# Sorting a graph's edges by source in lanes of four instead of two, with nine of sixteen tiles picked on the tensor engine

## The chip, the cores and the metric

The kernel runs on one core of a Trainium2 chip. The metric is the device time of one execution in microseconds. The profile is of one execution on the same core.

## The reference, cut to what matters

There are 8192 nodes with 128 features and 262144 edges. An edge has a source `src` (uniform at random), a destination `dst`, a weight and nine attributes; the edges come sorted by `dst`, whose density falls with the node's number (`8192 * u ** 2`).

```python
def _L0_gnn_ref(x, edge_row, edge_col, edge_vals, W):      # src, dst, edge_weight
    gathered = x[edge_col] * edge_vals[:, None]
    pre_embed = jax.ops.segment_sum(gathered, edge_row, num_segments=N)
    return pre_embed @ W.T
...
x = _layernorm(x + _L0_gnn_ref(x, src, dst, edge_weight, L0_gnn_W), axis=-1)
x = _layernorm(x + _L1_gnn_ref(x, edge_index, edge_attr_9, ...), axis=-1)
```

The first layer reads rows of `x` at `dst` and sums them at `src`, so it goes against the order in which the edges come. The second layer reads at `src`, forms a tensor product with the nine attributes, and sums at `dst`, in the order given.

## The kernel before, in words

The edges are seen as 128 rows of 2048. Row r holds edges r * 2048 onward; it is laid into a lane (a partition) so that lanes 2c and 2c + 1 hold row c and row 127 - c (`constants`, L124). Five blocks of code follow each other, with all engines meeting between them.

**Setup** (`setup`, L201 to L481). The rows are loaded by three indirect transfers of POOL, which then clears the accumulator `acc` (L283). DVE casts source and destination to floats (L350), builds the sort key (source above destination, L354 to L357), and measures each lane's range of destinations; PE mirrors these ranges between the two lanes of a pair (L446). DVE then makes the tables of the second layer (`layer1_tables`, L294 to L341) and the node numbers that a pair can reach (`node_f`, L423 to L426).

**Sort** (`first_edges`, stages on DVE L773 to L817). Each lane sorts its 2048 keys by a network of compare stages. A stage is a maximum (L805), a comparison (L806), a minimum (L809) and two predicated copies that move the weights along (L814, L817), all on DVE; ACT saves the lower weights and moves the higher keys (L695, L699). Stages go down to distance 4 in four interleaved runs, then merge these down to distance `FINEST` = 2. Then the two lanes of a pair are merged once: SP swaps their keys and weights (L651, L654), DVE keeps the smaller keys in one lane and the larger in the other (L795 to L801), and four cleaning stages at distance 1024 to 128 follow. Odd lanes hold their keys negated. Meanwhile POOL gathers the rows of `x` that each pair can reach, ACT and PE split them into three bf16 parts (`split_step`, `keep_left`).

**First layer.** Each lane's sorted edges are 16 tiles of 128, 2048 tiles in all. Tile t of every pair is handled for one lane and then the other, in eight groups of eight tiles each: 256 groups. The loop runs over t, and its body holds 16 groups, written out. For each tile PE sums `rows^T @ hot` into PSUM, where `hot` (128 x `WIN0` = 360 nodes) has the edge's weight at its source, and the place of the 360 columns within 3 banks is a register loaded from `starts_row` (L1102). The rows come in two ways. In each group of eight, tiles 0, 2, 4 and 6 (`FETCHED`) are picked from the split rows held on chip: PE spreads the destinations over the partitions (`spread`, L1050), ACT copies them and makes `rest_hot` (L725 to L731), DVE makes `near_hot` (L894), PE multiplies three bf16 parts by `near_hot` and one by `rest_hot` (`fetch`, L1065, L1067), ACT copies the result to `msg` (L737). Tiles 1, 3, 5 and 7 are gathered by POOL straight from memory (L989) into a ring of 16 slots, at most four groups ahead. DVE makes the `hot` products (L902) and, when a half is done, adds its three banks to `acc` (L915). On PE the order of a step is written out by hand:

```python
spread(k + 2, ...)
fetch(k + 1, (j + 1) % GROUPS)
sums(k, w, t, s, j)
```

If a tile's sources span more than `WIN0`, or the starts of one tile number lie too far apart, or the destinations of a pair more than `SPAN`, a flag turns on and the loop runs over all nodes in windows instead (`n_pass`).

**Norm, second layer, norm** (`norm_stage`, `layer1`). In the second layer POOL gathers one tile of rows at a time (L1375) into a ring of 16, and the sums and products of PE and DVE follow it.

Of the kernel before, what the change touches and what calls it, by code (L numbers as in the profile page):

```python
# [36 lines left out]
P = 128  # L37
# [11 lines left out]
WIN0 = 360  # L49
BANKS = 3  # L50
STEP = 512 - WIN0
RUNS = 4
FINEST = 2
REACH = (BANKS - 1) * STEP + 512
NOWHERE = 16384.0
GROUP = 8
FETCHED = (0, 2, 4, 6)
GATHERS = (1, 3, 5, 7)
KIND = (0, 1, 0, 1, 0, 1, 0, 1)
FEATS = 16  # L60
GATHERED = 4
SUMMED0 = 18
SPAN = 160
# [3 lines left out]
PAIRS = P // 2  # L67
X_PAIRS = [c for c in range(PAIRS) if c % GROUP in FETCHED]
# [12 lines left out]
C_ROW = C_SWAP + P  # L81
C_UPPER = C_ROW + 1
C_SIGN = C_UPPER + 1
C_PLACE = C_SIGN + 1
C_WANTED = C_PLACE + 2
C_ALL = C_WANTED + 2

# [15 lines left out]
def constants(n_nodes):  # L103
# [22 lines left out]
    c[lane ^ 1, C_SWAP + lane] = 1.0  # L126
    c[:, C_ROW] = row
    c[:, C_UPPER] = lane % 2
    c[:, C_SIGN] = 1.0 - 2.0 * (lane % 2)
    spare = lane < 3 * (SPAN - P)  # L130
    c[:, C_PLACE] = lane
    c[:, C_PLACE + 1] = np.where(spare, P + lane % (SPAN - P), P)
    c[:, C_WANTED] = lane - CENTER
    c[:, C_WANTED + 1] = np.where(spare, P + lane % (SPAN - P) - CENTER, -1000)
# [7 lines left out]
def gnn_kernel(nc, x, src, dst, attr, weight, w_lin, w_tp, consts, out, tables, x1):  # L142
# [8 lines left out]
    with ExitStack() as ctx:  # L151
        def sb(name, shape, dt):
            return ctx.enter_context(nc.sbuf_tensor(name, shape, dt))

        g.cst = sb("cst", [P, C_ALL], F32)
        g.ident_bf = sb("ident_bf", [P, g.RN + 1], BF16)
        g.acc = sb("acc", [P, g.N + REACH], F32)
# [8 lines left out]
        g.mix = sb("mix", [P, NA, D], F32)  # L166
        g.dst_rel = g.dst_col
# [4 lines left out]
        with ExitStack() as mid:  # L172
# [6 lines left out]
            g.node_f = sm("node_f", [P, 2, PAIRS], F32)  # L179
# [21 lines left out]
def setup(nc, g, src, dst, weight, w_lin, w_tp, consts):  # L201

    RN, TN = g.RN, g.TN
    with ExitStack() as ctx:
# [17 lines left out]
        g.tile_start = sb("tile_start", [P, TN], F32)  # L222
        row_no = sb("row_no", [P, 1], I32)
        turn_bf = sb("turn_bf", [P, P], BF16)
        lanes = sb("lanes", [P, 2, 2], F32)
# [4 lines left out]
        shown_in = sb("shown_in", [P, 3, PAIRS], F32)  # L230
        w_scalar = sb("w_scalar", [P, MUL], F32)
        w_vec = [sb(f"w_vec{i}", [P, MUL], F32) for i in range(2)]
        off_f = sb("off_f", [P, TN], F32)
        word_f = sb("word_f", [P, TN // QUAD_TILES], F32)
# [18 lines left out]
        pool_turn = sem("setup_pool_turn")  # L253
# [5 lines left out]
        l1_step = sem("l1_step")  # L259
# [6 lines left out]
        def _(sp):  # L266
# [3 lines left out]
            loads = [(w_scalar, w0, w3), (w_vec[0], w1, w2), (w_vec[1], w1, w4)]  # L270
# [6 lines left out]
        def _(pool):  # L277
            pool.wait_ge(row_no_made, 1)
            pool.sem_inc(pool_turn, 1)
# [3 lines left out]
            nc.gpsimd.memset(g.acc[:], 0.0)  # L283

        @block.vector
        def _(dve):
# [6 lines left out]

            def layer1_tables(dve):  # L294

                TN, Q, R = g.TN, QUAD_TILES, ROW_TILES
                l1_steps = [0]

                def link(ins):

                    l1_steps[0] += 1
                    ins.then_inc(l1_step, 1)
                    dve.wait_ge(l1_step, l1_steps[0])
# [1241 lines left out]
```

## Time and profile before

| | us |
|---|---|
| median of 3 runs | 4782.76 (4782.1 to 4785.0) |
| the profiled execution, its own time | 4778.88 |
| its span, first to last instruction | 4777.1 |
| PE busy in the span | 3699.2 (77%) |
| POOL busy | 3114.5 (65%) |
| DVE busy | 2246.6 (47%) |
| ACT busy | 1123.9 (24%) |

The span has a clear order: setup to 60 us, sort to 489, first layer to 2101, norm to 2155, second layer to 4723, norm to the end. Shares over the whole span mix these. Times of rows are in microseconds from the span's start; a row of the timeline merges instructions of one kind that follow each other, with their count after the x. Matmuls are pipelined: their starts tell the pace, their durations overlap.

### The profile page before, as it was taken

How to read it: one execution, taken by the hardware profiler on the slowest of the kernel's cores; microseconds unless marked ns; L12 is line 12 of the kernel's file. 1: busy time of each engine (PE TensorE's matmuls, PEld its weight loads, DVE VectorE, ACT ScalarE, POOL GpSimd, SP SyncE). 2: the span in 40 equal slices, each digit the busy share in tenths (PEclk: the TensorE clock that was granted, in tenths of full speed). 3: DMA queues.
4: the chain of work that ended last, by engine and by line, in shares of the span. 5: the costliest groups of instructions: out<-in, count | busy, mean ns of one | idle time of the engine just before them, and what ended most of it. 6: DMA issues, size and time to landing. Idle time of an engine off the chain costs nothing. (4 is left out here: it accounts for less than half of the span.)

```text
span 4777.1 us, 70528 instructions
## 1 busy us (share of the span) xinstructions
PE 3699.2 (77%) x17795; PEld 2639.9 (55%) x17796; DVE 2246.6 (47%) x4407; ACT 1123.9 (24%) x1890; POOL 3114.5 (65%) x3160
## 2 busy tenths in 40 slices
PE   1210999999999999987777777777777777777775
PEld 1000666666666666665555555555555555555554
DVE  8999555555555555562333333333333333333334
ACT  2442433333333333341111111111111111111102
POOL 3300666666666666637777777777777777777773
PEclk6555999999999999986777777777777777777776
DMA  1000111111111111122222222222222222222223
GB/s 44 17 5 18 42 42 42 42 42 42 42 42 42 42 42 42 42 85 59 55 56 56 56 56 56 56 56 56 56 56 56 56 56 56 56 56 56 56 56 97
DMA packets 115386, 238.26 MB, mean 50 GB/s; under 512 B 54001, under 2 KB 54145, under 8 KB 114705
## 3 DMA queue, kind: packets, MB, share of 16 engines
q0 software_dynamic: 100784, 208.87, 16.4%
q1 hardware_dynamic: 9954, 20.54, 1.4%
q10 hardware_dynamic: 4608, 8.39, 0.5%
q8 instruction: 16, 0.26, 0.0%
q14 instruction: 24, 0.20, 0.0%
HBM read 227.09 MB, written 8.40 MB: 49 GB/s over the span
## 5 line engine op out<-in xcount | busy, mean ns | idle before, releaser
L1375 POOL DMA_INDIRECT feat<-x,ids x2048 | 1933.2, 944 | 636.5 <-issue 568.2
L989 POOL DMA_INDIRECT l_feat<-in_x,id_of x1024 | 1081.9, 1057 | 724.7 <-PE l_pre L1093 258.1
L1439 PE MATMUL quad<-attr_hot,feat 128*128 128x144 f32 x4096 | 990.8, 360 | 417.2 <-DMA feat<-x,ids 410.9
L1481 DVE TENSOR_TENSOR group<-group,quad 128x504 f32 (+1 forms) x512 | 348.0, 680 | 1685.6 <-PE quad L1439 1685.6
L1439 PEld LDWEIGHTS quad<-attr_hot,feat 128*128 128x128 f32 x4096 | 660.2, 215 | 743.5 <-issue 716.0
L1446 PE MATMUL mixed<-group,mix 128*128 128x192 f32 x2304 | 693.4, 487 | 130.7 <-DVE group L1481 130.7
L1446 PEld LDWEIGHTS mixed<-group,mix 128*128 128x128 f32 x2304 | 651.3, 306 | 175.0 <-DVE group L1481 175.0
L1399 ACT CAST ids<-src_col 128x8 int32 x256 | 50.5, 197 | 2288.8 <-DMA feat<-x,ids 2288.8
L894 DVE TENSOR_SCALAR near_hot<-place,cst 128x512 bf16<-128x512 bf16 x256 | 90.5, 353 | 666.2 <-ACT place L725 666.2
L725 ACT CAST place<-place_b 128x512 bf16<-128x512 f32 x256 | 149.8, 585 | 948.2 <-PE place_b L1050 948.2
L1467 DVE TENSOR_TENSOR attr_hot<-hot,attr_t 128x1152 f32<-128x1152 f32 x256 | 346.8, 1355 | 45.9 <-DVE hot L1461 22.4
L1093 PE MATMUL l_pre<-keys,msg 128*128 128x360 f32 x768 | 307.9, 483 | 0.1
L1093 PE MATMUL l_pre<-w_row,l_feat 128*128 128x360 f32 x768 | 295.1, 466 | 0.0
L1093 PE MATMUL l_pre<-pad,msg 128*128 128x360 f32 x768 | 295.1, 466 | 0.0
L902 DVE TENSOR_SCALAR w_row<-swap,src_of,w_of 128x360 f32<-128x360 f32 x640 | 264.8, 463 | 1.9 <-PE l_pre L1093 1.9
L1065 PE MATMUL got<-x_near,near_hot 128*128 128x128 bf16 x3072 | 257.3, 220 | 1.3 <-ACT rest_hot L731 0.8
L902 DVE TENSOR_SCALAR keys<-swap,src_of,w_of 128x360 f32<-128x360 f32 x640 | 252.1, 460 | 0.0
L902 DVE TENSOR_SCALAR pad<-swap,src_of,w_of 128x360 f32<-128x360 f32 x640 | 251.8, 459 | 0.0
L1431 PE MATMUL quad<-zero_bf 1*128 1x504 bf16 x512 | 204.2, 399 | 51.2 <-issue 49.5
L1067 PE MATMUL got<-x_rest,rest_hot 128*128 128x128 bf16 x1024 | 224.8, 220 | 0.0
L1065 PEld LDWEIGHTS got<-x_near,near_hot 128*128 128x128 bf16 x3072 | 215.4, 98 | 2.1 <-issue 1.9
L1395 ACT ACTIVATE group<-group 128x1728 uint32<-128x1728 uint32 x128 | 210.3, 1643 | 13.8 <-issue 13.8
(235 smaller groups left out, 3978.0 us busy)
## 6 DMA issues: line engine op xcount, KB each, us to landing
feat<-x,ids POOLq DMA_INDIRECT x2048, 2.5
l_feat<-in_x,id_of POOLq DMA_INDIRECT x1024, 2.7
attr_in<-in_edge_attr SPq DMA_DIRECT2D x129, 72.0 KB
norm_x<-in_x SPq DMA_DIRECT2D x16, 256.0 KB, 2.6
x<-norm_z ACTq DMA_DIRECT2D x16, 256.0 KB, 2.4
norm_x<-x SPq DMA_DIRECT2D x16, 256.0 KB, 2.7
out<-norm_z ACTq DMA_DIRECT2D x16, 256.0 KB, 2.4
l_feat<-in_x,node POOLq DMA_INDIRECT x64, 2.6
```

The lines of the kernel that those rows point to most:

```text
L902: made = nc.vector.tensor_scalar(hot_of[(j % 2) * GROUP + i], iota[KIND[i]], src_of[s][:, c:c + 1], w_of[s][:, c:c + 1], ALU.is_equal, ALU ...
L989: pool.indirect_dma_start(feat[:, slot, :], None, x, bass.IndirectOffsetOnAxis(ap=id_of[s][:, c:c + 1], axis=0)).then_inc(feat_in[slot], 16)
L1065: nc.tensor.matmul(to, near_hot[z][:, m * P:(m + 1) * P], x_near[:, a, part, :], start=(part == 0), stop=False)
L1067: last = nc.tensor.matmul(to, rest_hot[z][:, m * P:(m + 1) * P], x_rest[:, a, :], start=False, stop=True)
L1093: made = nc.tensor.matmul(pre[:, s, bass.ds(places[i], WIN0)], rows, hot_of[(j % 2) * GROUP + i], start=False, stop=(j == GROUPS - 1 and i ...
L1375: pool.indirect_dma_start(feat[:, t, :], None, x1, bass.IndirectOffsetOnAxis(ap=ids[t // H][:, t % H:t % H + 1], axis=0),).then_inc(feat_i ...
L1395: nc.scalar.memzero(group[z][:]).then_inc(group_zero, 1)
L1431: nc.tensor.matmul(quad[:, q, 0:NA * QUAD_WIN], zero_bf[0:1, 0:P], zero_bf[0:1, :], start=True, stop=False, skip_group_check=True)
L1439: nc.tensor.matmul(bank[:, :, bass.ds(off, WIN)], feat[:, t, :], attr_hot[t // H][:, t % H, :, :], start=False, stop=(t % Q == Q - 1), ski ...
L1446: last = nc.tensor.matmul(mixed[:, z, 0:GROUP_WIN], g.mix[:, m, :], group[z][:, m, :], start=(m == 0), stop=(m == NA - 1))
L1467: nc.vector.tensor_tensor(attr_hot[h][:], hot[:].unsqueeze(2).to_broadcast(s4), by_tile[:, h * H:h * H + H, :].unsqueeze(3).to_broadcast(s ...
L1481: nc.vector.tensor_tensor(to, to, quad[:, q, 0:NA * QUAD_WIN].rearrange("p (m n) -> p m n", m=NA), ALU.add).then_inc(quad_added, 1)
```

## The change

- **Lanes merged four by four.** `MERGED` = 4. After the pair merge and a sign flip (`C_FLIP`) nine cleaning stages (distance 1024 down to `CLEANEST` = 4) sort each lane again; then lane v meets lane 3 - v of its quad, and then lane 1 - v; the four cleaning stages 1024 to 128 stay. `FINEST` is 4, so the two stages at distance 2 go.
- **Spans of 184 columns.** `WIN0` is 184, and all starts of one tile number and lane lie within one bank of 512 columns, so `pre` is one bank per part, cleared once and added once. A part is now 32 tiles, four groups; the loop body is again 16 groups.
- **Nine of sixteen tiles picked.** Groups take turns with five and four picked tiles; three and four are gathered, ring of 14 slots, at most four groups ahead. A quad reaches 288 nodes instead of 160, so a picked tile takes six matmuls with two `near_hot` and one with `rest_hot`.
- **Moved.** `layer1_tables` goes from setup to the start of the second layer's DVE code, `acc` is cleared by ACT instead of POOL. Setup mirrors the ranges twice. Buffers of the sort are used again for picks, messages and products.

```diff
-WIN0 = 360
-BANKS = 3
+WIN0 = 184
+BANK = 512
-FINEST = 2
+FINEST = 4
+CLEANEST = 4
-FETCHED = (0, 2, 4, 6)
-GATHERS = (1, 3, 5, 7)
+FETCHED = ((0, 2, 4, 6, 7), (1, 3, 5, 6))
+GATHERS = ((1, 3, 5), (0, 2, 4, 7))
+RING = 14
-SPAN = 160
+SPAN = 288
+MERGED = 4
...
 # setup
-            nc.gpsimd.memset(g.acc[:], 0.0)
...
+            link(nc.vector.tensor_copy(lanes[:, 3, :], pb[:, 0, 2:4]))
+            link(nc.vector.tensor_tensor(lanes[:, 0, 0:1], lanes[:, 2, 0:1], lanes[:, 3, 0:1], ALU.min))
+            link(nc.vector.tensor_tensor(lanes[:, 0, 1:2], lanes[:, 2, 1:2], lanes[:, 3, 1:2], ALU.max))
+            dve.sem_inc(lanes_made, 1)
+            dve.wait_ge(lanes_mirrored, 2)
...
-            layer1_tables(dve)
+            dve.wait_ge(weights_in, 16 * 12)
...
         @block.scalar
         def _(act):
+            nc.scalar.memzero(g.acc[:]).then_inc(acc_zero, 1)
...
 # first_edges
+    cleans = [(d, d) for d in (n // 2 >> i for i in range(n.bit_length())) if d >= CLEANEST]
     blocks = [(d, d) for d in (n // 2, n // 4, n // 8, P)]
+    merges = stages + cleans + blocks
...
+            sp.wait_ge(low_made, n_clean)
+            sp.wait_ge(high_moved, n_clean)
+            for v in range(L):
+                sp.dma_start(far_keys[v:P:L, :], g.keys[3 - v:P:L, :]).then_inc(far_keys_in, 16)
+            sp.wait_ge(w_moved, 2 * n_clean)
+            for v in range(L):
+                sp.dma_start(far_w[v:P:L, :], g.w_row[3 - v:P:L, :]).then_inc(far_w_in, 16)
+            sp.wait_ge(keys_merged, 4)
+            for v in range(2):
+                sp.dma_start(far_keys[v:P:2, :], g.keys[1 - v:P:2, :]).then_inc(far_keys_in, 16)
+            sp.wait_ge(merged, 2)
+            for v in range(2):
+                sp.dma_start(far_w[v:P:2, :], g.w_row[1 - v:P:2, :]).then_inc(far_w_in, 16)
...
+                    dve.wait_ge(keys_merged, 1)
+                    nc.vector.tensor_scalar(g.keys[:], g.keys[:], g.cst[:, C_FLIP:C_FLIP + 1], None,
+                                            ALU.mult).then_inc(keys_merged, 1)
...
+                if s == n_clean:
+                    for m in (2, 3):
+                        landed = (0, 0, 96, 128)[m]
+                        dve.wait_ge(far_keys_in, landed)
+                        nc.vector.scalar_tensor_tensor(swap[:], far_keys[:], -1.0, g.keys[:], ALU.mult,
+                                                       ALU.is_lt).then_inc(compared, 1)
+                        dve.wait_ge(compared, s + m)
+                        nc.vector.scalar_tensor_tensor(g.keys[:], far_keys[:], -1.0, g.keys[:], ALU.mult,
+                                                       ALU.min).then_inc(keys_merged, 1)
+                        dve.wait_ge(keys_merged, 2 * m - 1)
+                        if m == 2:
+                            nc.vector.tensor_scalar(g.keys[:], g.keys[:], g.cst[:, C_SIGN:C_SIGN + 1], None,
+                                                    ALU.mult).then_inc(keys_merged, 1)
+                        dve.wait_ge(far_w_in, landed)
+                        nc.vector.copy_predicated(g.w_row[:], swap[:], far_w[:]).then_inc(merged, 1)
...
-                nc.vector.tensor_scalar(near_hot[z][:], place[z][:], wanted, None, ALU.is_equal).then_inc(near_made, 1)
+                used = NF[z] * P
+                nc.vector.tensor_scalar(near_hot[z][0][:, 0:used], place[z][:, 0:used], wanted[0], None, ALU.is_equal)
+                nc.vector.tensor_scalar(near_hot[z][1][:, 0:used], place[z][:, 0:used], wanted[1], None,
+                                        ALU.is_equal).then_inc(near_made, 1)
...
-                for b in range(BANKS):
-                    dve.wait_ge(added, h * BANKS + (2 * BANKS + b))
-                    to = g.acc[:, bass.ds(at + b * STEP, 512)]
-                    nc.vector.tensor_tensor(to, to, pre[:, s, b * 512:(b + 1) * 512], ALU.add).then_inc(added, 1)
+                dve.wait_ge(added, h + 2)
+                to = g.acc[:, bass.ds(at, BANK)]
+                nc.vector.tensor_tensor(to, to, pre[:, s % 2, :], ALU.add).then_inc(added, 1)
...
 # POOL
-                                pool.wait_ge(summed, k * 2 + (SUMMED0 - 2 * (FEATS // NG) + 2))
+                                pool.wait_ge(summed, k + (SUMMED0 - AHEAD + 1))
...
+                    pool.wait_ge(summed, (wd * PS + ws) * (R * PER) + (R * PER + SUMMED0))
+                    for some in (feat_in[0:RING // 2], feat_in[RING // 2:RING]):
+                        pool.inc_swdge_sem(some, [R * USES * 16] * len(some), mode="sub")
+                    pool.sem_inc(landings_cleared, 1)
...
 # PE
-                    for part in range(3):
-                        nc.tensor.matmul(to, near_hot[z][:, m * P:(m + 1) * P], x_near[:, a, part, :],
-                                         start=(part == 0), stop=False)
+                    for c in range(2):
+                        for part in range(3):
+                            nc.tensor.matmul(to, near_hot[z][c][:, m * P:(m + 1) * P], x_near[:, a, 3 * c + part, :],
+                                             start=(c == 0 and part == 0), stop=False)
...
+                    pe.wait_ge(landings_cleared, w + 1)
...
 # layer1, DVE
+            layer1_tables(dve)
             nc.vector.memset(zero_bf[:], 0.0).then_inc(zero_made, 1)
```

The order of PE's instructions in one step of the first layer's loop. Before, a step of eight tiles, four of them picked (`place_b` is the spread, `got` the fetch, `l_pre` the sums; ISA and REGISTER_ALU rows are waits and address steps):

```order
L1050 MATMUL place_b<-pos,ident_bf 128x128 x4
L1057 REGISTER_ALU
L1065 MATMUL got<-x_near,near_hot 128x128 x3
L1067 MATMUL got<-x_rest,rest_hot 128x128
...
L1102 ISA
L1102 TENSOR_LOAD starts_row
...
L1093 MATMUL l_pre<-w_row,msg 128x360
L1093 ISA
L1093 MATMUL l_pre<-w_row,l_feat 128x360
```

In the changed kernel, a step with five picked tiles (`near_hot` lies in `far_w`, `rest_hot` in `far_keys`, `msg` in `pad`):

```order
L1057 MATMUL place_b<-pos,ident_bf 128x128 x5
L1064 REGISTER_ALU
L1073 MATMUL got<-x_near,far_w 128x128 x6
L1075 MATMUL got<-x_rest,far_keys 128x128
...
L1106 ISA
L1106 TENSOR_LOAD starts_row
...
L1098 MATMUL l_pre<-keys,pad 128x184
L1098 ISA
```

The order of spread, fetch, load of the starts and sums is the same; a picked tile has seven fetches instead of four, and a sum 184 columns instead of 360.

On DVE, after the last stage in a lane of the changed kernel (the merge of the pair, then the first cleaning stage):

```order
L779 SCALAR_TENSOR_TENSOR swap<-keys,far_keys 128x2048
L782 SCALAR_TENSOR_TENSOR keys<-keys,far_keys 128x2048
L785 TENSOR_SCALAR keys<-keys,cst 128x2048
L788 COPY_PREDICATED w_row<-swap,far_w 128x2048
L809 TENSOR_TENSOR pad<-keys 128x1024
L810 TENSOR_TENSOR swap<-keys 128x1024
L813 TENSOR_TENSOR keys<-keys 128x1024
L818 COPY_PREDICATED w_row<-swap,w_row 128x1024
L821 COPY_PREDICATED w_row<-swap,pad 128x1024
```

and behind the nine cleaning stages, before the four that were there:

```order
L795 SCALAR_TENSOR_TENSOR swap<-far_keys,keys 128x2048
L798 SCALAR_TENSOR_TENSOR keys<-far_keys,keys 128x2048
L802 TENSOR_SCALAR keys<-keys,cst 128x2048
L805 COPY_PREDICATED w_row<-swap,far_w 128x2048
L795 SCALAR_TENSOR_TENSOR swap<-far_keys,keys 128x2048
L798 SCALAR_TENSOR_TENSOR keys<-far_keys,keys 128x2048
L805 COPY_PREDICATED w_row<-swap,far_w 128x2048
```

Seven passes over all 2048 columns are new here, one above, and 45 half-length ones in the cleaning stages.

## Rows read from the trace of the kernel before

**Rows 1.** Windows: length; busy us (instructions) of PE, PEld, DVE, ACT, POOL; PEclk.

```profile
1004.08:1104.45 100.37, 100.36 (x583) 66.93 (x582) 58.05 (x150) 39.44 (x70) 67.34 (x64) 1.00 0.15 42
500.00:600.00 100.00, 99.91 (x582) 66.61 (x581) 55.93 (x147) 39.44 (x70) 77.75 (x74) 1.00 0.18 49
...
2160.00:4700.00 2540.00, 1945.61 (x7988) 1476.14 (x7988) 787.26 (x1145) 255.78 (x381) 1920.10 (x2035) 0.75 0.21 56
```

**Rows 2.** Timeline of PE: start, us, engine, line, op, operands, count.

```profile
1003.47 0.77 PE L1093 MATMUL l_pre<-w_row,l_feat 128*128 128x360 f32 x2
1004.08 0.39 PE L1050 MATMUL place_b<-pos,ident_bf 128*128 x4
...
1005.14 0.22 PE L1067 MATMUL got<-x_rest,rest_hot 128*128 128x128 bf16 x1
1005.33 0.87 PE L1093 MATMUL l_pre<-w_row,msg 128*128 128x360 f32 x2
...
1104.45 0.39 PE L1050 MATMUL place_b<-pos,ident_bf 128*128 x4
```

**Rows 3.** Timeline of PE in the second layer, sums of 144 columns.

```profile
3008.16 1.25 PE L1439 MATMUL quad<-attr_hot,feat 128*128 128x144 f32 x8
...
3009.65 0.51 PE L1439 MATMUL quad<-attr_hot,feat 128*128 128x144 f32 x2
```

**Rows 4.** Timelines of DVE and POOL in the first layer.

```profile
1005.39 1.97 DVE L902 TENSOR_SCALAR keys<-swap,src_of,w_of 128x360 f32<-128x360 f32 x5
...
1006.30 1.19 POOL L989 DMA_INDIRECT l_feat<-in_x,id_of  x1 [0.30 <-issue]
```

**Rows 5.** Timeline of DVE and SP at the end of the sort.

```profile
423.00 2.43 DVE L814 COPY_PREDICATED far_w<-swap,far_w 128x1022 f32<-128x1022 int32 x1
...
424.33 1.18 SPq L651 DMA_DIRECT2D keys<-far_keys  x2
...
428.66 2.29 DVE L795 SCALAR_TENSOR_TENSOR swap<-keys,far_keys 128x2048 int32<-128x2048 f32 x1 [0.71 <-DMA keys<-far_keys]
...
433.20 2.45 DVE L801 COPY_PREDICATED w_row<-swap,far_w 128x2048 f32<-128x2048 int32 x1
...
448.50 1.23 DVE L805 TENSOR_TENSOR pad<-keys 128x1024 f32<-128x1024 f32 x1
...
454.88 1.23 DVE L805 TENSOR_TENSOR pad<-keys 128x1024 f32<-128x1024 f32 x1
...
461.26 1.29 DVE L831 TENSOR_SCALAR keys<-keys,cst 128x2048 f32<-128x2048 f32 x1
```

**Rows 6.** Timeline of the setup, and a transfer's time to landing.

```profile
8.65 7.62 POOL L283 MEMSET acc<- 128x9008 f32 x1
10.75 7.73 DVE L350 CAST rows_f<-rows_i 128x2048 f32<-128x2048 int32 x2 [6.27 <-DMA rows_i<-in_src,row_no]
...
45.59 0.46 DVE L308 TENSOR_TENSOR mix<-w_scalar,cst 128x288 f32<-128x288 f32 x1 [0.16 <-DVE shown_in L415]
...
57.84 0.28 DVE L423 TENSOR_SCALAR node_f<-pb,cst 128x64 f32<-128x64 f32 x1
...
rows_i<-in_dst,row_no POOLq DMA_INDIRECT x1, 7.7
```

**Rows 7.** Timeline at the first layer's start and end.

```profile
489.55 0.60 PE L1050 MATMUL place_b<-pos,ident_bf 128*128 128x128 bf16 x4 [6.98 <-issue]
...
496.36 0.82 PE L1078 MATMUL l_pre<-zero_row 1*128 1x512 bf16 x3
...
2098.77 2.37 DVE L915 TENSOR_TENSOR acc<-acc,l_pre 128x512 f32 x3 [7.72 <-PE l_pre L1093]
```

**Rows 8.** Timeline at the second layer's start.

```profile
2157.28 0.95 POOL L1375 DMA_INDIRECT feat<-x,ids  x1 [12.64 <-issue]
...
2164.85 0.59 PE L1431 MATMUL quad<-zero_bf 1*128 1x504 bf16 x1
```

**Rows 9.** Transfer queues, 486 to 590 us: packets, MB, share.

```profile
q8 instruction: 6, 0.10, 0.4%
```

More of the change, by code:

```diff
@@ L66 @@
 KEY_BIT = 30
-PAIRS = P // 2
-X_PAIRS = [c for c in range(PAIRS) if c % GROUP in FETCHED]
+MERGED = 4
+QUADS = P // MERGED
+TURNS = 3
+X_QUADS = [c for c in range(QUADS) if c % GROUP in FETCHED[c // GROUP % 2]]
+FILLED = 20
 WIN = 16
@@ L129, in constants @@
     c[:, C_SIGN] = 1.0 - 2.0 * (lane % 2)
[L130 to L134, printed above, removed]
+    c[:, C_FLIP] = np.array([1.0, -1.0, -1.0, 1.0])[lane % MERGED]
+    spare = lane < 3 * REST
+    for k in range(2):
+        c[:, C_PLACE + k] = k * P + lane
+        c[:, C_WANTED + k] = k * P + lane - CENTER
+    c[:, C_PLACE + 2] = np.where(spare, 2 * P + lane % REST, 2 * P)
+    c[:, C_WANTED + 2] = np.where(spare, 2 * P + lane % REST - CENTER, -1000)
     return c.astype(np.float32)
@@ L563, in first_edges @@
[L563 to L567 removed]
+        iota = [dst_f[:, k * WIN0:(k + 1) * WIN0] for k in range(3)]
+        node = sb("node", [P, 3, QUADS], I32)
@@ new lines, in first_edges @@
+        x_near = sb("x_near", [P, FILLED, 6, D], BF16)
+        x_rest = sb("x_rest", [P, FILLED, D], BF16)
+        spare = [half for buf in (far_w, far_keys) for half in (buf[:].bitcast(BF16),)]
+        picks = [buf[:, i * MOST * P:(i + 1) * MOST * P] for buf in spare for i in range(6)]
+        near_hot = [picks[0:2], picks[2:4]]
+        place, rest_hot, rest_far = picks[4:6], picks[6:8], picks[8]
+        msg = [pad[:, i * MOST * D:(i + 1) * MOST * D].rearrange("p (a d) -> p a d", a=MOST) for i in range(2)]
@@ new lines, in first_edges @@
+        feat = sb("l_feat", [P, 2 * RING, D], F32)
+        ones, minus = feat[:, 2 * RING - 1, :], feat[:, 2 * RING - 2, 0:P // 2].bitcast(BF16)
+        first, last = feat[:, 2 * RING - 3, 0:R], feat[:, 2 * RING - 3, R:2 * R]
+        rows_in = [[feat[:, (3 * z + c) * STAGED:(3 * z + c + 1) * STAGED, :] for c in range(3)] for z in range(2)]
+        zero_bf = pad[:, 2 * MOST * D:2 * MOST * D + 256].bitcast(BF16)
+        hot_of = [buf[:, i * WIN0:(i + 1) * WIN0] for buf in (g.keys, g.w_row) for i in range(GROUP)]
@@ L769, in _ @@
         def _(dve):
-            nc.vector.tensor_scalar(node[:], g.node_f[:], g.N - 1.0, None, ALU.min).then_inc(nodes_made, 1)
-            nc.vector.memset(zero_bf[:], 0.0)
-            nc.vector.tensor_scalar(minus[:], g.cst[:, C_IDENT:C_IDENT + P], -1.0, None, ALU.mult).then_inc(minus_made, 1)
-            for s, (p, k) in enumerate(stages + blocks):
+            nc.vector.tensor_scalar(node[:], g.node_f[:], g.N - 1.0, None, ALU.min).then_inc(begun, 1)
+            nc.vector.tensor_scalar(minus[:], g.cst[:, C_IDENT:C_IDENT + P], -1.0, None, ALU.mult).then_inc(begun, 1)
+            for s, (p, k) in enumerate(merges):
                 keys, w = buffers(s)
@@ L824, in link @@
                 dve.wait_ge(step, steps[0])
-            n_all = len(stages + blocks)
+            n_all = len(merges)
             dve.wait_ge(high_moved, n_all)
```

563 lines of the change are left out of this document (273 added, 290 removed).

## The prediction, written before the changed kernel was run

> **What bounds the kernel now.** I read the windows view first, because it cuts the span into stages with a bound each. In the first layer's loop (sixteen groups of eight tiles from 1004.08 to 1104.45) PE is busy 100.36 of 100.37 us, DVE 58.05, ACT 39.44 and POOL 67.34, with the clock granted in full; in the second layer POOL is busy 1920 of 2540 us, nearly the same share, but PE is not full (1946) [rows 1]. POOL's own row there explains it: 2035 gathers in 2540 us are one every 1.25 us, of which 0.94 is work and 0.30 the issue of the next [rows 1], and they never stop, so 2048 take 2560 us. So three stages matter: setup and sort (to 489 us), where DVE has no idle time; the first layer (to 2101 us), bound by PE; and the second layer, bound by POOL's gathers, which the change leaves alone.
>
> One group of the first layer, from the timeline [rows 2]: 4 spread and 16 fetch matmuls of 128 bf16 columns start between 1004.08 and 1005.14 (19 steps of 0.056 us), the sums start at 1005.33, and the next same-numbered group of the loop's next turn stands at 1104.45. That is 100.37 / 16 = **6.27 us a group**. A tile's fp32 sum of 360 columns is two matmuls in the trace: two start at 1003.47 and the next row at 1004.08, so 0.3025 us apart and 0.605 a tile. Eight sums 4.84, twenty bf16 matmuls 1.11, leave 0.23 for the place where PE's queue loads the eight starts, and 0.09 for clearing three banks once in eight groups.
>
> **The first layer, part by part.** 256 groups remain.
> - *Sums, 360 to 184 columns.* The trace has no 184. Rows of 144 columns at the full clock: eight in 1.25 us, two in 0.51, so (1.25 - 0.51) / 6 = 0.123 us apart [rows 3]. A line through 144 (0.123) and 360 (0.3025) gives 0.1565, so 0.313 us a tile; bounds are the 144-column price (0.247) and the 360-column one. Eight: 2.50 us, against 4.84.
> - *Fetches.* 4.5 tiles of eight instead of 4, each with seven matmuls instead of four, and 4.5 spreads: 36 bf16 matmuls at 0.0556 = 2.00 us, against 1.11.
> - *Gap and clearing.* The queue's load is unchanged, 0.23; one bank once in four groups, 0.07 with its wait.
> - Sum: 2.50 + 2.00 + 0.23 + 0.07 = **4.80 us a group**. Saved: 256 x 1.47 = **-377 us**.
>
> Who could keep PE from it? DVE's products stand 0.377 us apart at 360 columns (five in 1.97) [rows 4]; by columns that is 0.19 at 184, bounds 0.19 to 0.38. Eight take 1.5 us (3.0 at worst). DVE's 58.05 / 16 = 3.63 us less 3.02 of products leave 0.61 for a pick and its share of the adds; two picks of nine eighths the width make that 1.4 at most: 2.9 us, at worst 4.4. ACT's 39.44 / 16 = 2.47 us grows by 9/8 to 2.8, plus staging. Both lie beside PE's 4.80. POOL is close. It issues 3.5 gathers a group. While it still filled its ring (500 to 600 us) it got 74 out in 100 us, 1.35 each [rows 1]; a gather that runs beside DVE's products takes 1.19 + 0.30 us [rows 4], against the second layer's 0.94 + 0.30. Products now cover 3.0 of 6.27 us and will cover 1.5 of 4.80, so two thirds of the extra 0.10 stays: 1.32 x 3.5 = **4.6 us**, bounds 4.4 (none slowed) and 5.2 (all slowed). I take 4.6, since 500 to 600 us is the same code under the same neighbours. PE stays the bound by 0.2 us, and costs of POOL are hidden for as long as that margin lasts.
>
> **Sort.** A full stage is 6.38 us (448.50 to 454.88) [rows 5]. Two stages of distance 2 go; there each of the two predicated copies takes 2.43 us (423.00) instead of 1.25, so a stage is 8.6: -17. Nine cleaning stages come, 1024 down to 4: 9 x 6.3 = +57. The pair merge (428.66 to 435.65, 0.7 us of waiting in front) gets a sign flip, a one-operand pass, 1.3 (461.26), and waits longer, because the keys' transfer (started 424.33, used 428.66, so 4.3 us) was covered by the slow copies: +3.5. The two merges of four lanes are new: a wait of 3.4 us for four transfers in a row, compare 2.3, minimum 2.2, flip 1.3, copy 2.45; then 2.4 of waiting (its transfer starts only after the flip), 2.3, 2.2, 2.45: +21. Behind each wait stands the rest of the sort, since DVE does all its compares. Bounds of the waits: 0 to 6 us each. Sum of the sort: **+65 us**.
>
> **Setup.** The tables of the second layer (mix at 45.59 to the node rows at 57.84) leave DVE: -12.2 [rows 6]. They go to the second layer's start. There DVE starts 12.2 us later, so the first four tiles, done about 2164.8 before, are done about 2177.1; POOL, which began at 2157.28, needs the first slot free after sixteen gathers, at 2177.3 [rows 8]. POOL is not held, so I cost it at nothing (0 to +4); after that PE has a quarter of its time free to catch up. The clearing of acc goes from POOL to ACT. DVE's two casts took 7.73 us from 10.75, while POOL's memset ran from 8.65 for 7.62 us; another one-operand pass over 2048 columns takes 1.3 (461.26) [rows 5]. With the memset gone the second cast waits for its own input only (issued 6.46, landing 7.7 later, 14.2), so it starts 3 us sooner: -3 (0 to -4). ACT's fill has no reader before the first turned column and is covered by the loads; if ACT's start were late it would cost up to 5. The lanes' extra exchange holds PE's tile starts: +2.1; node numbers +0.6. Sum: **-12.5 us**.
>
> **Entry and end of the first layer.** From the first spread to the first sums 6.8 us passed, at half clock [rows 7]; 35 instead of 16 fetches, twice, and longer passes on ACT: +3.5. At the end one add instead of three (2.37 us): -1.7. The new wait of PE ahead of its loop (on landings_cleared) is met by POOL's first increment in the sort, and POOL's two subtractions of semaphores after the last sum run beside that add: 0 (to +2).
>
> **Sum.** -12.5 + 65 + 3.5 - 377 - 1.7 = -323 us. From the profiled execution's 4778.9: 4456; the median of the runs is 3.9 us above it, so **4460 us**.
>
> **The rivals.**
> A. *PE's loop no longer stays resident.* In the first turn of the loop the queue that carries PE's code fetched six blocks of 16 KB; from 600 to 1990 us it fetched none, so fourteen turns ran from what was held [rows 9]. A turn has 583 + 582 matmuls and weight loads [rows 1] and some 270 waits, loads and address steps, 1435; afterwards 16 x 52 + 4 = 836 of each and the same rest, 1940, so about eight blocks. If that is too much, each of the 15 jumps back waits for a transfer. The shortest gathers here land in about 2.5 us, and the sixteen matmuls of a group's sums stand in PE's queue as cover: 0 to 3 us each, 0 to +45 us, 4456 to 4505. Half and half that it is fetched again; that it costs more than 15 us, 0.15. The Trainium skill ("Runtime: NRT & Kernel Launch", Instruction fetch mechanics) gives PE 2048 instructions in blocks of 256 and says that a taken branch outside the window stalls; by that, 1940 instructions lie over eight or nine blocks and would be fetched again each turn. Its further remark that the window is two blocks does not agree with this trace, where six were held.
> B. *POOL becomes the bound.* At 1.49 us for every gather a group takes 5.2 us: +0.4 x 256, 4560. For it: the small margin. Against it: a product that is half as long covers less of a gather. Middle case 5.0 us: 4510. Chance 0.12.
> C. *The clock falls, and the kernel is slower than before.* In the second layer, where PE pauses for data every group, the granted clock is 0.75 of full [rows 1]. At half clock a group's 4.57 us of matmuls take 9.1, +4.6 us a group. If PE waited often enough (case B is how it would begin) for that to hold in 70 of 256 groups, the gain of 323 us is gone; from there on it is slower, and at half clock throughout the time is 5630. Against it: PE's own gap is 0.23 of 6.27 now and 0.23 of 4.80 afterwards. Chance 0.03.
> D. *The short path isn't taken.* If a tile's edges spanned more than 183 nodes, or a lane group's starts more than 328, the kernel would fall back to 45 passes. By the reference's inputs the widest tile after this sort spans 179, the starts 198 and the two ranges of a quad together 262 of 286. Chance below 0.01.
>
> **How the numbers follow.** Main case 0.69 (4443 to 4475: the sums' price within 0.003 us either way, 4096 of them, makes 12, the merges' waits and the moved tables the rest), A dearly 0.15, B 0.12, C and D 0.04. The range 4436 to 4535 leaves out C, D, most of B's dear end and a cheap surprise. A measurement of this kernel tells 0.2%, some 10 us, from no change. Only C and D lead to no gain: faster 0.95, same 0.01, slower 0.04.
>
> **What would show it.** The windows view of the first layer: PE full, clock 1.00, sixteen groups in 77 us. Sums 0.157 us apart. Of POOL's idle time before gathers a part still ends with PE; if all of it is issue, B holds. Code packets of 16 KB all through the layer show A, and its price is the step from the last sum of a turn to the next spread. DVE's sort ends some 53 us later than before. The second layer takes 2560 us again. It is wrong if PE has idle time inside the loop, or if products stay 0.38 apart.

## The result and the profile after

| | before | after |
|---|---|---|
| time, median of 4 runs | 4782.43 us (4779.62 to 4785.0) | 4498.65 us (4495.43 to 4502.99) |
| ratio | | 0.9407 (95%: 0.9391 to 0.9424) |
| the profiled execution's span | 4777.1 us | 4493.6 us |
| first spread of the first layer | 489.55 | 539.88 |
| first layer, from there to the first matmul of norm0 | 1612.6 us | 1273.8 us |
| second layer, first gather to last | 2556.1 us | 2559.5 us |

The change saves 284 us where 323 were forecast, so the time is inside the range but 39 us above the figure. Almost all of what is missing lies in the first layer, which was to get 375 us shorter and got 339.

The windows view of the kernel after. The first two answer to the first layer's loop of before and to the second layer [rows 1]; the last two are a piece of 3.4 us and a piece without a jump. Columns as in [rows 1].

```profile
1004.53:1104.60 100.07, 95.76 (x1012) 90.48 (x1011) 65.83 (x204) 53.85 (x94) 66.48 (x71) 0.98 0.18 48
...
1900.00:4400.00 2500.00, 1915.15 (x7894) 1455.44 (x7893) 773.38 (x1125) 251.78 (x375) 1889.89 (x2003) 0.75 0.21 56
...
1025.10:1028.50 3.40, 3.40 (x22) 2.77 (x20) 3.08 (x10) 2.38 (x6) 1.88 (x2) 0.50 0.21 59
1029.00:1100.00 71.00, 71.00 (x784) 67.78 (x783) 48.82 (x150) 40.80 (x69) 47.38 (x50) 1.00 0.17 47
```

PE is still what bounds the layer: it is busy 71.00 of 71.00 us between two jumps. But over a stretch with a jump in it, 4.3 us of 100 are idle, and the granted clock is 0.98 in place of 1.00. For 3.4 us behind the jump it was 0.50, the lower of its two levels, 1.2 GHz.

This is the jump, in the timeline of PE of the kernel after: the last sums of a turn, the spread that is the loop body's first work, the next sums; then, from 1044.38, the same spread and sums inside a turn, without a jump ahead of them. A row of x2 is one tile's sum.

```profile
1020.74 0.79 PE L1098 MATMUL l_pre<-w_row,pad 128*128 128x184 f32 x4
1021.36 0.47 PE L1098 MATMUL l_pre<-w_row,l_feat 128*128 128x184 f32 x2
...
1023.87 0.45 PE L1057 MATMUL place_b<-pos,ident_bf 128*128 x5 [2.03 <-issue]
...
1026.65 0.60 PE L1085 MATMUL l_pre<-pad 1*128 1x512 bf16 x1
1027.18 0.98 PE L1098 MATMUL l_pre<-keys,pad 128*128 128x184 f32 x2
...
1044.38 0.47 PE L1098 MATMUL l_pre<-w_row,l_feat 128*128 128x184 f32 x2
1044.70 0.44 PE L1057 MATMUL place_b<-pos,ident_bf 128*128 x5
...
1046.63 0.39 PE L1085 MATMUL l_pre<-pad 1*128 1x512 bf16 x1
1046.95 0.58 PE L1098 MATMUL l_pre<-keys,pad 128*128 128x184 f32 x2
```

Inside a turn the spread follows the last sum's start by 0.32 us. At the jump it follows by 2.51, of which 2.03 are idle, and no engine released it ("issue"). The first tile's sum behind it takes 0.98 us at the half clock, and 0.58 inside the turn. The loop runs 15 turns, so there are 14 jumps back; the sixteenth turn is written out behind it. From the spreads' starts of all groups: at a jump the step from one spread to the next is 7.0 to 7.8 us in place of 4.91; most turns take 78.7 to 79.3 us, every third 80.5 to 81.2, and the loop's last turn, with no jump behind it, 76.8. The 14 turns that end in a jump together take 39.7 us more than 76.8 each. In the kernel before, all 15 turns end in a step of 6.18 to 6.21 us, as long as the steps ahead of it, with a jump or without.

What was fetched meanwhile, from the DMA view of the kernel after, 600 to 1700 us. The stretch of before had no such queue at all; its first turn had six packets [rows 9].

```profile
q0 software_dynamic: 24779, 50.82, 17.1%
q8 instruction: 125, 2.05, 0.8%
```

125 packets of 16 KB in some 13.9 turns are nine a turn. The loop's code comes from memory again in every turn. Counted in the two traces, a turn of the loop is 1,432 instructions of PE before and 1,919 after.

### The profile page after: what moved, and what is told of

Its sections match the earlier page's. It is cut to its first block and busy times, and to the rows that moved or that the text cites. A ratio compares the mean times of both kernels' runs of the same rounds, so it can differ in the third digit from the quotient of the medians.

```text
span 4493.6 us, 78519 instructions
## 1 busy us (share of the span) xinstructions
PE 3325.0 (74%) x21856; PEld 2742.6 (61%) x21858; DVE 2216.3 (49%) x4679; ACT 1222.0 (27%) x1998; POOL 2873.1 (64%) x3027
## 5 line engine op out<-in xcount | busy, mean ns | idle before, releaser
L991 POOL DMA_INDIRECT l_feat<-in_x,id_of x896 | 848.1, 947 | 746.5 <-ACT w_of L701 347.6
L1073 PE MATMUL got<-x_near,far_w 128*128 128x128 bf16 x6912 | 481.9, 220 | 1.7 <-ACT far_keys L714 1.1
L1073 PEld LDWEIGHTS got<-x_near,far_w 128*128 128x128 bf16 x6912 | 437.3, 98 | 4.0 <-issue 2.5
L902 DVE TENSOR_SCALAR keys<-swap,src_of,w_of 128x184 f32<-128x184 f32 x1024 | 325.4, 387 | 0.0
L902 DVE TENSOR_SCALAR w_row<-swap,src_of,w_of 128x184 f32<-128x184 f32 x1024 | 318.9, 380 | 0.5 <-PE l_pre L1098 0.5
L1098 PE MATMUL l_pre<-keys,pad 128*128 128x184 f32 x1280 | 297.7, 331 | 0.0
L1098 PE MATMUL l_pre<-w_row,l_feat 128*128 128x184 f32 x1024 | 255.7, 331 | 0.3
L1075 PE MATMUL got<-x_rest,far_keys 128*128 128x128 bf16 x1152 | 253.6, 220 | 0.0
L1098 PEld LDWEIGHTS l_pre<-keys,pad 128*128 128x128 f32 x1280 | 212.3, 191 | 17.3 <-issue 15.3
L1098 PE MATMUL l_pre<-w_row,pad 128*128 128x184 f32 x1024 | 222.2, 319 | 0.0
```

The lines of the kernel that those rows point to most:

```text
L902: made = nc.vector.tensor_scalar(hot_of[(j % 2) * GROUP + i], iota[KIND[j % 2][i]], src_of[s % 2][:, c:c + 1], w_of[s % 2][:, c:c + 1], AL ...
L991: pool.indirect_dma_start(feat[:, landing % RING, :], None, x, bass.IndirectOffsetOnAxis(ap=id_of[s % 2][:, c:c + 1], axis=0)).then_inc(fe ...
L1073: nc.tensor.matmul(to, near_hot[z][c][:, m * P:(m + 1) * P], x_near[:, a, 3 * c + part, :], start=(c == 0 and part == 0), stop=False)
L1075: last = nc.tensor.matmul(to, rest_hot[z][:, m * P:(m + 1) * P], x_rest[:, a, :], start=False, stop=True)
L1098: made = nc.tensor.matmul(pre[:, s % 2, bass.ds(places[i], WIN0)], rows, hot_of[(j % 2) * GROUP + i], start=False, stop=(j == GROUPS - 1 a ...
```

## The experiments

All times are medians, beside the kernel before on the same chip. The twelve runs fell on chips of two kinds. For two of them the kernel before took 4781 us. For ten it took 5319 to 5332 us, and there the engines behind TensorE were released late (last part of this section). Only the two of the first kind can be set against the 4498.65 us above. Of the other traces I use single steps, at which PE waited for no other engine.

**Half a turn as PE's loop body (e1_half, e1b_half_again).** The same work in the same order; PE's body holds 8 groups (1,020 instructions) and runs twice a turn.

```diff
-                    v = (j * GROUP + i) * L + s
-                    lane = g.ident_bf[:, v:v + 1].to_broadcast([P, P])
+                    v = s + (j * GROUP + i) * L
+                    lane = g.ident_bf[:, bass.ds(v, 1)].to_broadcast([P, P])
...
                     with pe.Fori(0, R - 1) as t:
-                        slots(t, False)
+                        with pe.Fori(0, 2) as half:
+                            half_turn(t, half)
```

> The changed kernel with one edit, on PE alone: its loop body is half a turn (eight groups), run twice for each of 15 turns in a nested loop, so that the body holds about half as many instructions; the same work, in the same order. Theory (PE's loop of some 1,860 instructions is fetched again at each jump, which costs 2.1 to 2.6 us there and another 1.6 us at every third turn, where the granted clock falls to half for 3.4 us): no 16 KB packets of PE's code queue from the second turn of the first layer on, steps of 4.8 us throughout, the first layer 36 to 39 us shorter, 4460 us in all (4455 to 4467). Rival (the missing 36 us are POOL's gathers or VectorE's products, which are late once in sixteen groups, where a turn's tables change): the jump is not the cause, the longer steps stay, 4495 to 4505, a little more for thirty jumps in place of fifteen.

> The kernel of e1_half again, because in the first four runs TensorE halted for 0.7 to 2 us at places where it waited for nothing, in both layers, and the kernel before took 5319 us beside it in place of 4782. Here the kernel before should take 4780 again. Theory (the jump to the loop's start, with code that has to be fetched): 4460 us (4455 to 4467), ratio 0.9325 to the kernel before, steps of 4.8 us, no long step at a turn's end. Rival (the long steps have another cause): 4495 to 4505, ratio 0.940 to 0.942.

Measured, the second time: 4484.8 us (4484.34 to 4485.43), ratio 0.9381 (0.9365 to 0.9396): 14 us less than the changed kernel, where the theory asked for 38 and the rival for none. The runs of the two don't overlap, though the intervals of their ratios just do (0.9391 and 0.9396). The trace parts theory and rival. The DMA view of the same 1100 us has no q8 row any more:

```profile
q0 software_dynamic: 25056, 51.36, 16.0%
q14 instruction: 3, 0.02, 0.0%
```

In the windows view PE is busy 1083 of 1100 us at a clock of 1.00:

```profile
600.00:1700.00 1100.00, 1083.13 (x11699) 1020.94 (x11697) 748.34 (x2293) 619.01 (x1063) 739.37 (x784) 1.00 0.16 47
```

And the timeline of PE at a turn's end has the spread 0.31 us behind the last sum (1097.80 to 1098.11), as inside a turn; the rows from 1722.22 on are the end of the loop and the start of the last turn:

```profile
1097.80 0.47 PE L1098 MATMUL l_pre<-w_row,l_feat 128*128 128x184 f32 x2
1098.11 0.44 PE L1057 MATMUL place_b<-pos,ident_bf 128*128 x5
...
1100.28 0.39 PE L1085 MATMUL l_pre<-pad 1*128 1x512 bf16 x1
...
1722.22 0.39 PE L1057 MATMUL place_b<-pos,ident_bf 128*128 x4
1724.72 0.57 PE L1098 MATMUL l_pre<-w_row,l_feat 128*128 128x184 f32 x2 [0.16 <-issue]
...
1727.31 0.44 PE L1057 MATMUL place_b<-pos,ident_bf 128*128 128x128 bf16 x5
...
1732.16 0.39 PE L1057 MATMUL place_b<-pos,ident_bf 128*128 128x128 bf16 x4
```

So the theory's three signs (fetches, long steps, the fallen clock) left together, at all 14 jumps. The rival falls: POOL, DVE and ACT do the same work at the same places. The jump from turn to turn isn't quite free: the step behind it takes 5.11 us (5.00 in the changed kernel) where others of its kind take 4.85.

What ate 28 of the 40 us is new: a turn of the loop takes 78.65 us and not 76.8, or 0.116 us more in each of 240 groups. Steps have to be compared at the same place of the turn. A step whose sums begin with the clearing of a bank takes 4.85 us in both kernels. The twelve others of a turn take 4.46 (with five spreads) and 4.91 (with four) in the changed kernel's loop, 4.61 and 5.06 in the half loop, and 4.39 and 4.80 in the last turn of either, which is written out. The half loop has 60 more instructions in eight groups than the changed kernel, nearly all of them register work, above all an address written ahead of every spread matmul (9 in two groups), since the column of the identity now depends on the half. The time doesn't appear at the spreads, which still take 0.39 us for four, but ahead of the group's first sum, which follows the last fetch by 0.34 us (the median of 112) in place of 0.19; at 1724.72 PE waits there 0.16 us for its own instructions. A loop without those registers was built (two loops, below).

**A coarser sort: FINEST 8 in place of 4.**

```diff
-FINEST = 4
+FINEST = 8
```

> The changed kernel with sorts and merges in a lane that stop at distance 8 in place of 4 (cleanings still go down to 4): two stages fewer, and tiles span at most 183 nodes by the lists of edges in place of 179, still under the 184 columns of a span. Theory (a stage costs what the trace of before shows for one of the sort's, 6.3 us, wherever it stands, and nothing else hangs on it): 12.5 us less, 4486 (4484 to 4489). Rival (the x rows' split between the stages, 45 steps that begin at stage 5, is then late and holds the sort or TensorE's start back): 0 to 5 us less. If a tile were too wide, the general path would take about three times as long, over 7000.

Measured: 4484.51 us (4479.6 to 4485.01), ratio 0.938 (0.9364 to 0.9396), 14.1 us less than the changed kernel. DVE's pair merge starts at 388.26 in place of 401.13 (12.9 us earlier for two stages, 6.4 each), and the first spread comes 13.1 us earlier. As expected. PE's loop is the same here and moves the same 125 packets, with a long step at each of the 14 jumps; the granted clock fell behind the 4th, 9th and 12th, so not at every third.

**Two loops, one for each half of the lanes.** Every engine walks all sixteen turns of lanes 0 and 1 of each four, then those of lanes 2 and 3; so PE's body is 8 groups with the identity's column fixed.

```diff
-                    with pe.Fori(0, R - 1) as t:
-                        slots(t, False)
-                    slots(R - 1, True)
+                    for half in range(2):
+                        with pe.Fori(0, R - 1) as t:
+                            slots(half, t, False)
+                        slots(half, R - 1, True)
```

> The changed kernel with the first layer's lanes walked in two passes over the turns: all sixteen turns of the first two lanes of each four, then all sixteen of the other two. Every engine's order is changed alike, the work is the same, and each loop body on TensorE holds 8 groups (some 930 instructions) with no register moved ahead of a spread, which the half loop had (4.5 a group, and 0.21 to 0.24 us a group with them). Theory (the long steps are the fetch behind the jump; the half loop gave 15 x 2.6 us back and lost 256 x 0.22 = 56 less what it hid in its registers): 4.80 us a group throughout, no 16 KB packet but in the first turns of each pass, the first layer 36 to 39 us shorter than the changed kernel's, 4462 (4457 to 4468). Rival (the group itself costs 0.2 us more in any short body, since something else of the half loop's made it): as the half loop, 4485.

> The kernel of e5_two_loops with FINEST 8 in place of 4, the two edits that each alone gave or should give time. If they add up, since one lies in the sort and the other in the first layer: 4462 - 14 = 4448 (4443 to 4455).

Both fell on chips of the second kind: 5443.34 us (5433.21 to 5447.72) beside 5331.65, and 5418.69 (5407.65 to 5437.98). The second was run twice more, 5414.0 beside 5323.94 and 5432.22 beside 5330.92. These times tell nothing apart. So the version that by the sum of its parts should stand some 50 us below the changed kernel has no undisturbed time. The two versions that have one beat both kernels by their medians: 4484.5 and 4484.8 us.

The traces do tell the theory from the rival, in the steps that nothing disturbed. The same step of the same turn, first in the two loops (963 instructions a body, not the 930 of the expectation), then in the half loop on such a chip: four spreads, the group's last fetch, its first sum, the next spread.

```profile
953.50 0.39 PE L1075 MATMUL place_b<-pos,ident_bf 128*128 x4
...
955.62 0.22 PE L1093 MATMUL got<-x_rest,far_keys 128*128 128x128 bf16 x1
955.81 0.57 PE L1116 MATMUL l_pre<-w_row,l_feat 128*128 128x184 f32 x2
...
958.41 0.44 PE L1075 MATMUL place_b<-pos,ident_bf 128*128 x5
```

```profile
964.25 0.39 PE L1057 MATMUL place_b<-pos,ident_bf 128*128 x4
...
966.37 0.22 PE L1075 MATMUL got<-x_rest,far_keys 128*128 128x128 bf16 x1
966.72 0.57 PE L1098 MATMUL l_pre<-w_row,l_feat 128*128 128x184 f32 x2
...
969.31 0.44 PE L1057 MATMUL place_b<-pos,ident_bf 128*128 x5
```

The two loops take 4.91 us, as the changed kernel does inside its turn, and the half loop 5.06. With five spreads the shortest steps are 4.46 and 4.62. So a short body as such costs nothing in these steps; the register work that came with the half does. And PE is never idle at the end of one of the two loops' turns, while its code queue moves 8 packets in 600 to 1700 us, so this kernel too has no refetch. That its time on an undisturbed chip would be the 4462 us of the expectation isn't shown.

**Three turns as the loop body, eight tiles picked, spans of 208 columns.** Three edits of the changed kernel, each alone: 5 jumps in place of 15 with all code fetched; four and four tiles picked in place of five and four; WIN0 = 208.

> The changed kernel with one edit, on PE alone: its loop body is three turns (48 groups, some 5,600 instructions), run five times. All of PE's code is fetched as before, but there are 5 jumps in place of 15. Theory (the price lies in the jump, where the fetch cannot run ahead of the engine, and straight code costs nothing): the long steps of 7.0 to 7.5 us come only at every third turn, 10 x 2.6 = 26 us less, 4470 (4465 to 4480). Rival (the fetching itself costs, wherever the code comes from memory): as the changed kernel, 4495 to 4503. Rival (the long step belongs to the turn's end: tables, or semaphores): the same, 4495 to 4503.

> The changed kernel with eight of sixteen tiles picked and eight gathered (five and four became four and four; a ring of 16 landing places). PE has 32 matmuls of 128 columns a group in place of 36 on the mean (0.22 us less, 4.58), POOL four gathers a group in place of 3.5. Theory (PE bounds the first layer of the changed kernel, and POOL at 3.5 x 1.25 = 4.37 us a group lies just under it): POOL becomes the bound at 4 x 1.25 = 5.0 us a group, PE idles before its sums for landings, and with some of PE's pauses the granted clock may fall more often: layer 1280 to 1320 us from first spread to norm, 4505 to 4545. Rival (PE's loop code is the whole of what is above 4.80 a group, and POOL is far from bounding): 256 x 0.22 = 56 us less, 4442 to 4450.

> The changed kernel with spans of 208 columns in place of 184, the rest alike. Theory (PE bounds every group by the columns it streams; a sum is 4 x 184 columns at the full clock or 0.313 us): a sum becomes 0.313 x 208 / 184 = 0.354 us, 8 x 0.041 = 0.33 us a group more, 256 groups: +84 us, 4575 to 4590. VectorE's products come 0.29 to 0.31 us apart where they were 0.286 (360 columns: 0.375 in the kernel before), 2.4 us a group, hidden; POOL's gathers stay at 0.95 us. Rival (part of the group is set by products or gathers that wait on one another, not by columns): less than half of that, +20 to +45.

These and the first half-turn run fell on one chip of the second kind. With the half turn at 5443.8 us: three turns 5411.12 (5392.1 to 5428.46), eight picked 5502.69 (5496.75 to 5504.92), 208 columns 5436.84 (5428.09 to 5453.83); the kernel before 5319.46. Again on another chip: three turns 5423.66, eight picked 5513.81, beside 5331.65. None of these times settles its question, since each expectation was for a time near 4500. The trace of three turns does settle one: whether the price lies in the jump or in the fetching. Its code queue moves 84 packets in 600 to 1700 us, nearly eight a turn, yet at the ten turn ends where straight code runs on, PE is never idle ahead of the spread, in either run. At the four real jumps it is idle for 0.14, 2.23, 0.37 and 0.10 us in the first run and for 2.19, 2.19, 0 and 0 in the second. With eight picked, which jumps back 14 times, it is idle at all 14, for 0.9 to 2.6 us. This is a turn end without a jump and one with it, in the second run of three turns:

```profile
768.72 0.47 PE L1098 MATMUL l_pre<-w_row,l_feat 128*128 128x184 f32 x2
769.03 0.44 PE L1057 MATMUL place_b<-pos,ident_bf 128*128 x5
...
870.21 0.47 PE L1098 MATMUL l_pre<-w_row,l_feat 128*128 128x184 f32 x2
872.88 0.45 PE L1057 MATMUL place_b<-pos,ident_bf 128*128 x5 [2.19 <-issue]
```

So the fetching alone costs nothing that shows, and the turn's end as such doesn't either. Why some jumps cost little on these chips stayed open, and so did whether POOL becomes the bound with eight picked. A sum of 208 columns starts 0.35 us behind the last, as expected:

```profile
1000.19 0.52 PE L1098 MATMUL l_pre<-keys,l_feat 128*128 128x208 f32 x2
1000.54 0.51 PE L1098 MATMUL l_pre<-keys,pad 128*128 128x208 f32 x2
```

and eight of DVE's products (first the kernel after, then the one with 208 columns) hardly feel the columns:

```profile
1041.36 2.51 DVE L902 TENSOR_SCALAR keys<-swap,src_of,w_of 128x184 f32<-128x184 f32 x8
```

```profile
1004.97 2.55 DVE L902 TENSOR_SCALAR keys<-swap,src_of,w_of 128x208 f32<-128x208 f32 x8
```

Counted in the trace, a turn is 1,791 instructions of PE with eight picked, and the page of that kernel still shows 144 packets of code. So bodies of 963, 1,020 and 1,432 instructions are held, and those of 1,791 and 1,919 are not. The expectations' 1,860 leaves out the 56 semaphore waits of a turn.

**What the chips of the second kind do.** The half-turn kernel ran on both, unchanged. Its windows, first where the kernel before took 4781 us, then where it took 5319: 60 to 400 us (sort), 600 to 1700 (first layer), 2600 to 4000 (second layer).

```profile
60.00:400.00 340.00, 46.16 (x59) 11.31 (x60) 320.98 (x303) 136.24 (x167) 68.66 (x54) 0.50 0.04 12
...
2600.00:4000.00 1400.00, 1070.64 (x4412) 813.07 (x4412) 433.22 (x630) 140.98 (x210) 1058.04 (x1123) 0.75 0.19 56
```

```profile
60.00:400.00 340.00, 46.16 (x59) 11.31 (x60) 320.44 (x303) 136.24 (x167) 68.42 (x53) 0.50 0.04 13
600.00:1700.00 1100.00, 904.10 (x8743) 834.88 (x8741) 556.30 (x1716) 462.13 (x796) 551.66 (x585) 0.92 0.13 35
2600.00:4000.00 1400.00, 881.74 (x3688) 727.59 (x3688) 354.51 (x523) 118.34 (x175) 883.77 (x936) 0.68 0.18 47
```

The sort, which is DVE's, is the same to 0.2%. The first layer takes 1704.7 us in place of 1262.5, the second 3066.8 in place of 2559.7. ACT's lines of the two first layers show where it is lost, first the undisturbed one:

```profile
L722 ACT COPY pad<-got 128x512 f32<-128x512 f32 x224 | 141.4, 631 | 2.9
```

```profile
L722 ACT COPY pad<-got 128x512 f32<-128x512 f32 (+1 forms) x167 | 105.3, 631 | 230.9 <-remote 169.8 <-PE got L1075 60.5
```

ACT's copy of the fetched rows starts 0.33 us behind the start of PE's last fetch matmul (the median of 256 groups); on the other chip it is 1.75 us, one time in ten 4.4 or more, and up to 7.5 past the first groups. PE's rows look as before when they run, but what waits for them is released late, by something that the profile doesn't name ("remote"), and then PE stands still in its turn. PE also stands idle ahead of its own sums for up to 1.8 us there with nothing that released it. That its results come late is a reading of these rows; what makes them late isn't shown. Of the kernel before there is no trace on such a chip, only the time: 540 us more. If its second layer lost the same 507 us, which no run shows, its first layer lost only some 30, where the half-turn kernel loses 442. On these chips every relative was slower than the kernel before, by ratios of 1.0172 to 1.0347. The changed kernel itself wasn't run on one.

## Why the prediction was right in its total and wrong in its likeliest case

The time lies in the stated range, but 39 us above the figure and 24 above the likeliest case (4443 to 4475). The range held because it took in most of what rival A could cost, and that was given a chance of 0.15.

**The group's price: right.** 4.80 us was the sum of its terms; the loop's last turn took 76.8 / 16 = 4.80. Two tiles' sums (x4) start at 1020.74 and the next at 1021.36, 0.31 us a tile, 0.313 forecast. The line through 144 and 360 columns carried, at 208 too. The gap of 0.23 us, carried over from the loop of before, holds the loop's own register work: written out, the same steps take 4.39 and 4.80 in place of 4.46 and 4.91.

**Rival A: the step that failed.** The prediction gave the fetched loop "half and half", but that "it costs more than 15 us, 0.15", because "the sixteen matmuls of a group's sums stand in PE's queue as cover", 0 to 3 us a jump. It happened, at 1.9 to 2.5 us a jump and 1.6 more where the clock fell, 39.7 us in all, nearly the whole 0 to 45. The cover was counted in matmuls and not in time. Eight sums of 184 columns are 2.5 us of work, and the fetch outlasted what of them was still queued by 2.03 us, the idle time at 1023.87. If the fetch began with the first of these sums, it took some 4.5 us, an estimate from those two rows, where 2.5 us of a gather's landing had been the measure. Second, a stall was priced as if nothing followed, but the clock fell to 0.50 behind 4 of the 14. The counts were nearly right: 1,435 and 1,940 instructions were taken where the traces have 1,432 and 1,919, and there are 14 jumps and not 15. The Trainium skill ("Runtime: NRT & Kernel Launch", Instruction fetch mechanics) gives PE room for 2,048 instructions, refilled in blocks of 256, and says that a taken branch to a target outside the current window of two blocks stalls. The trace agrees on the blocks and on the stall, with nine packets of 16 KB a turn for a body of 1,919. It doesn't agree on the window, since bodies of 1,432 and 1,020 ran without a packet.

**Rival B: didn't happen.** POOL's gathers take 946 ns in the loop (775 of them), not longer, so 1.25 us each and 4.4 us a group, the lower bound and not the 4.6 taken. The extra 0.25 us of the kernel before belonged to products of 360 columns beside a gather: in its loop the gathers with DVE's products beside them throughout took 1.18 us (232 of them) and those with none 0.94 (225). With products of 184 columns it is 0.95 and 0.94. The line view of POOL, 600 to 1700 us, shows that PE releases it for a good part of its idle time:

```profile
L991 POOL DMA_INDIRECT l_feat<-in_x,id_of x775 | 733.5, 946 | 367.3 <-issue 190.4 <-PE l_pre L1098 165.9 <-ACT w_of L701 11.0
```

**DVE and ACT.** Products were to stand 0.19 us apart "by columns"; they stand 0.30 apart ((2.51 - 0.38) / 7), against 0.38 at 360 columns, so they have a fixed part. DVE is busy 66% of the loop, 3.25 us a group where 2.9 was forecast (at most 4.4); ACT 54%, 2.7 for 2.8. Both stayed hidden, as priced.

**Rival C** appears in small: 3.4 us of half clock at 4 of 14 jumps, a 0.98 in the window, not 70 groups.

**Setup and sort: right, within 2 us.** DVE's merges in the timeline of the kernel after, with the last cleaning ahead of them [rows 5]:

```profile
401.13 2.29 DVE L779 SCALAR_TENSOR_TENSOR swap<-keys,far_keys 128x2048 int32<-128x2048 f32 x1 [2.97 <-DMA keys<-far_keys]
...
453.96 1.23 DVE L809 TENSOR_TENSOR pad<-keys 128x1024 f32<-128x1024 f32 x1
...
460.21 1.23 DVE L809 TENSOR_TENSOR pad<-keys 128x1024 f32<-128x1024 f32 x1
...
469.31 2.29 DVE L795 SCALAR_TENSOR_TENSOR swap<-far_keys,keys 128x2048 int32<-128x2048 f32 x1 [2.98 <-DMA far_keys<-keys]
...
479.52 2.29 DVE L795 SCALAR_TENSOR_TENSOR swap<-far_keys,keys 128x2048 int32<-128x2048 f32 x1 [1.94 <-DMA far_keys<-keys]
...
486.70 1.23 DVE L809 TENSOR_TENSOR pad<-keys 128x1024 f32<-128x1024 f32 x1
```

Setup ends 12.2 us earlier (48.39 for 60.58; -12.5 forecast), with the second cast at 13.86 in place of 17.27. The compare of the pair merge, 428.66 before, comes 27.5 earlier: 12.2 of setup, less 2.3 of longer wait (2.97 for 0.71), leaves 17.6 for the two stages of distance 2 (-17). A cleaning is 6.25 us (453.96 to 460.21; 6.3). The two merges of four lanes last from 466.3 to 486.7, 20.4 us (+21), with waits of 2.98 and 1.94 (3.4 and 2.4). The first spread comes 50.3 us later; -12.5 + 65 was 52.5.

**The small terms.** From the first spread to the first clearing of a bank 9.7 us pass, +2.9 (+3.5). From the last sum to the norm's first matmul 2.9 us pass, 1.2 less than before (-1.7). The second layer takes 3.4 us more (0, up to +4): its first gather took 2.21 us, and after that it is POOL's pace again.

## What to carry to other kernels

Count the instructions of a loop body for each engine before and after a change, and look in the trace at whether the engine's code queue moves packets in the steady loop; where a body no longer stays held, it pays at every jump, in time that the work in the queue covers only if it lasts longer than the fetch (here 2.5 us of short sums did not). Splitting the loop so that the body is held again gave 11 us of the layer's 40 back. The split had put a register write ahead of each short matmul, and the two loops, which need none, ran their undisturbed steps 0.15 us faster. And time a change on more than one chip: the same half-turn kernel stood at 0.938 and at 1.024 of the kernel before.

## What the runs showed of the hardware that was not expected

- PE keeps a loop body of 1,432 instructions and fetches one of 1,791 or more again in each turn; straight-line code is fetched too, and costs nothing that the trace shows (ten turn ends without a jump, none idle, with nearly eight packets a turn).
- After a pause of some 2 us at a jump the granted clock fell to 0.50 for 3.4 us, but not at each: at every third jump of the changed kernel (4 of 14), and with FINEST = 8, which leaves PE's loop as it is, at the 4th, 9th and 12th. With the pauses gone it stayed at 1.00 through the loop.
- A gather on POOL took 1.18 us beside DVE's products of 360 columns and 0.95 beside products of 184.
- DVE's products of 184, 208 and 360 columns stand 0.30, 0.31 and 0.38 us apart: half the columns save a fifth of the time.
- A register write ahead of each short matmul of PE cost 0.15 us in each step of eight tiles that doesn't clear a bank, and it shows ahead of the first sum, not at the short matmuls.
- On some chips the engines behind TensorE were released late, by up to 7.5 us where 0.33 is usual, at rows of TensorE that look normal, while DVE's sort took the same time. What makes a chip so stayed open.
